# Relative attention: one written order for TensorE, one accumulator for a head, four fold buffers

## What is computed

```python
idx = clip(k - q, -64, 64) + 64                      # 129 relative positions
rk, rv = embK[idx], embV[idx]
logits = einsum('bhqd,bhkd->bhqk', q, k) + einsum('bhqd,qkd->bhqk', q, rk)
w = softmax(logits)
out = einsum('bhqk,bhkd->bhqd', w, v) + einsum('bhqk,qkd->bhqd', w, rv)
x = x + out @ Wo.T + bo
```

## Time and profile before

| | |
|---|---|
| median of 3 runs | 4228.33 us (4212.84 to 4229.1) |
| profiled execution, its own time | 4235.89 us |
| its span | 4234.1 us |
| mean granted TensorE clock | 0.953 |
| PE busy, DVE, ACT, POOL | 92%, 81%, 69%, 35% of the span |

### The profile page before, as it was taken

The page is one execution under the profiler, slowest core; times in us unless marked ns, Lnnn a source line. Parts: engine busy times, 40 slices in busy tenths (PEclk is TensorE's granted clock), DMA queues, the critical chain, the costliest instruction groups (busy, mean ns, idle before and its releaser), DMA issues. The chain is left out here.

```text
span 4234.1 us, 77590 instructions
## 1 busy us (share of the span) xinstructions
PE 3900.7 (92%) x26574; PEld 2061.0 (49%) x26574; DVE 3421.2 (81%) x6363; ACT 2918.5 (69%) x5867; POOL 1485.5 (35%) x1459
## 2 busy tenths in 40 slices
PE   9699999999999999997879999999999999769998
PEld 5255554455544555543533333333333333659998
DVE  7788888888888888880778999999898994557776
ACT  4078777788777887885216777777777777336666
POOL 0356666666666666663100001010000010533233
PEclk9599999999999999998978999999999999779999
DMA  8656666677666666662673334243433331679997
GB/s 309 166 146 171 166 158 160 156 169 171 167 164 164 171 162 165 159 149 86 234 191 53 62 64 72 54 72 61 64 63 63 60 61 41 160 281 325 321 326 223
DMA packets 478603, 635.62 MB, mean 150 GB/s; under 512 B 61320, under 2 KB 404088, under 8 KB 464000
## 3 DMA queue, kind: packets, MB, share of 16 engines
q1 hardware_dynamic: 459680, 607.31, 55.9%
q0 software_dynamic: 18528, 23.34, 2.9%
HBM read 413.23 MB, written 216.19 MB: 149 GB/s over the span
## 5 line engine op out<-in xcount | busy, mean ns | idle before, releaser
L396 DVE TENSOR_REDUCE pa_pm<-pa_psA 128x2 f32<-128x1024 f32 x1024 | 1208.5, 1219 | 136.5 <-PE pa_psA L472 136.3
L1095 ACT ACTIVATE ra_p<-ra_psS 128x512 f32<-128x512 f32 x2048 | 1082.1, 605 | 323.8 <-PE ra_psS L1172 231.6
L444 ACT ACTIVATE pa_p<-pa_psS 128x512 f32<-128x512 f32 x2048 | 1063.8, 603 | 277.4 <-PE pa_psS L490 273.4
L1006 DVE TENSOR_REDUCE ra_pm<-ra_psA 128x1 f32<-128x896 f32 x1024 | 1113.4, 1087 | 162.0 <-PE ra_psA L1130 145.5
L490 PE MATMUL pa_psS<-pa_qs,pa_zs 50*128 50x512 f32 x2048 | 799.4, 467 | 70.9 <-ACT pa_p L444 40.6
L472 PE MATMUL pa_psA<-pa_zs,pa_qs 48*128 48x512 f32 x2048 | 802.8, 475 | 32.8 <-DMA pa_zs<-k_halves 18.2
L1130 PE MATMUL ra_psA<-ra_zs,ra_qs 48*128 48x512 f32 x2048 | 737.0, 454 | 20.6 <-DVE ra_pm L1008 9.9
L1172 PE MATMUL ra_psS<-ra_qs,ra_zs 50*128 50x512 f32 (+3 forms) x2176 | 705.4, 410 | 27.6 <-ACT ra_p L1095 17.9
L490 PEld LDWEIGHTS pa_psS<-pa_qs,pa_zs 50*128 50x128 f32 x2048 | 342.0, 185 | 624.0 <-ACT pa_p L444 611.5
L1203 PE MATMUL ra_psO<-ra_p,ra_vs 128*32 128x512 f32 (+3 forms) x6400 | 557.2, 453 | 0.0
L1172 PEld LDWEIGHTS ra_psS<-ra_qs,ra_zs 50*128 50x128 f32 x2176 | 354.7, 188 | 410.0 <-ACT ra_p L1095 312.7
(11 more groups left out here) (243 smaller groups left out, 4853.6 us busy)
## 6 DMA issues: line engine op xcount, KB each, us to landing
mo_w_parts<-second_weight_parts SPq DMA_DIRECT2D x39, 2048.0 KB, 9.0
relative_rows<-ra_rst SPq DMA_DIRECT2D x128, 512.0 KB, 4.1
ra_blk<-window_rows SPq DMA_DIRECT2D x128, 512.0 KB, 5.0
ra_zs<-k_halves SPq DMA_DIRECT2D x192, 248.0 KB, 7.5
mo_w_raw<-ffn_W SPq DMA_DIRECT2D x39, 1024.0 KB, 11.5
ra_dl<-relative_rows SPq DMA_DIRECT2D x128, 256.0 KB, 5.5
window_rows<-ra_pc SPq DMA_DIRECT2D x128, 256.0 KB, 4.5
pa_qs<-q_halves SPq DMA_DIRECT2D x192, 128.0 KB, 6.5
```

Of the source, the lines that this page charges most:

```text
L396: dve.reduce_max(pm[:, par, 2 * a:2 * a + 2], psA[w][:, :, :], AX.X).then_inc(s_am.h, 1)
L444: act.activation(pr[:, i % NPR, :], psS[:, slot(i), :], ACT.Exp).then_inc(s_ex.h, 1)
L1006: dve.reduce_max(pm[:, q, i, 2 * left:2 * left + 1], psA[w][:, lo:lo + 2 * G - P], AX.X).then_inc(s_far.h, 1)
L1095: act.activation(dst, psS[:, slot(i), :], ACT.Exp if kind == "E" else ACT.Copy).then_inc(s_cp.h, 1)
```

## The change

TensorE's order becomes a written string for each step. `RING` is built from a string of kinds: each step takes four banks of four different chunks, so that column tile c of `psO` belongs to chunk c and adds up over all 16 steps of a head. The last step also multiplies `evc` with `ptr` into the same tiles. `evacuate`, `gather_heads`, `sel`, `ot` and VectorE's `keep_head` go; ScalarE copies `psO` once a head. W and F banks are spread over the head, at 12, 19, 20, 28, 33, 42, 49, 51 and 34, 48, 53, 67. `blk_p` has four buffers, `ob` two; `psS` slots go round by three across heads too. Transfers, joins and folds stand in a new order, those of chunk 0 of head t+1 now in head t.

```diff
-R_STEPS = (1, 2, 3, 5)
-F_STEP = 2
-RTURNS = TURNS + 1 + len(R_STEPS)
-WX_STEPS = (8, 10, 10, 10, 12, 13, 13, 14, 14, 14, 15, 17, 21, 22, 22, 23)
-REL_AHEAD, REL_LEAD = 18, 7
-REL_ORDER = "saasOsaas"
-RC_REL = 30
-SUM_TURNS = (13, 18, 23, 28)
+REL_STEPS = ("sRO", "asasssaaRsssO", "saaassasaasO", "sasasaaO", "saasO", "saasassaO", "assaaasssasaO", "asssaRsO",
+             "saassRO", "asaassasO", "MsssaassaasasaO", "aassaasO", "asassasaO", "aassaasO", "asasssaassasaO",
+             "saasasaOsaas")
+RING_KINDS = "EEEEEEEEEEEEWEEEEEEWWEEEEEEEWEEEEWFEEEEEEEWEEEEEFWEWEFEEEEEEEEEEEEEF"
+WX_AT = (38, 41, 42, 45, 52, 55, 58, 72, 75, 85, 87, 89, 89, 90, 92, 95)
+REL_AHEAD, REL_LEAD = 19, 9
+RC_REL = 7
+SUM_TURNS = ((1, 24), (0, 1), (0, 10), (0, 18))
+RTURNS = TURNS + 4
...
-        blk_p = sb("blk", [P, 2, 4, W])
+        blk_p = sb("blk", [P, 4, 4, W])
-        recb, ob = sb("recb", [P, UN, G]), sb("ob", [P, UN, G])
+        recb, ob = sb("recb", [P, UN, G]), sb("ob", [P, 2, UN, G])
...
@@ SyncE, a head @@
+                    write_p(t, p, 1)
+                    if divide:
+                        store_denominators(t, n)
+                    if third:
+                        write_r(t + 2, p, 0)
+                    read_p(t, p, 1)
+                    if divide:
+                        read_denominators(n)
+                    if third:
+                        write_r(t + 2, p, 1)
+                    if more:
+                        load_stack(t + 1, p + 1, 64, s_qe, STEPS * t)
+                    if p == 2 and third:
                         load_v(t + 2, 4 * (t + 2))
+                    if third:
                         read_r(t + 2, p, 0)
+                    write_p(t, p, 2)
+                    if divide:
+                        store_reciprocals(n)
+                    if third:
                         read_r(t + 2, p, 1)
                     read_p(t, p, 2)
+                    if divide:
                         spread_reciprocals(n)
                     if t + 3 < HEADS:
                         s_am.wait(sp, 32 * (t + 2))
                         load_stack(t + 3, p + 1, 0, s_qa)
+                    write_p(t, p, 3)
+                    if third:
+                        write_r(t + 2, p, 2)
+                        write_r(t + 2, p, 3)
+                    read_p(t, p, 3)
+                    if more:
+                        send_m(t + 1, p + 1)
+                    if third:
+                        read_r(t + 2, p, 2)
+                    if more:
+                        write_p(t + 1, p + 1, 0)
+                    if third:
+                        read_r(t + 2, p, 3)
+                    if more:
+                        read_p(t + 1, p + 1, 0)
+                    if divide:
                         store_o(t, n)
...
@@ GpSimd, a head @@
+                    if more:
                         lay_v(t + 1, p + 1, it + 1 + (p + 1) // U)
+                    join_p(t, p, 2)
+                    fold_p(t, 1)
+                    if third:
                         part_r(t + 2, 0)
                     join_p(t, p, 3)
+                    if third:
                         part_r(t + 2, 1)
+                    fold_p(t, 2)
+                    if more:
+                        join_p(t + 1, p + 1, 0)
+                    fold_p(t, 3)
+                    if p % 2 == 0 and n >= 0:
+                        divide(n)
+                    if third:
                         part_r(t + 2, 2)
                         part_r(t + 2, 3)
+                    if more:
+                        fold_p(t + 1, 0)
+                        join_p(t + 1, p + 1, 1)
...
@@ ScalarE @@
-            def evacuate(t, c):
-                s_us.wait(act, STEPS * t + 4 * c + 4)
-                s_fm.wait(act, t + 1)
-                act.activation(ot[:, c * G:(c + 1) * G], psO[:, :], ACT.Copy).then_inc(s_oev.h, 1)
+            def keep_head(t):
+                s_us.wait(act, STEPS * (t + 1))
+                s_ob.wait(act, 64 * (t // UN - 1))
+                act.activation(ob[:, t // UN % 2, t % UN, :], psO[:, :], ACT.Copy).then_inc(s_nf.h, 1)
...
@@ TensorE @@
-                s_cp.wait(pe, NR * t + before(i) + 1)
+                s_cp.wait(pe, NR * t + i - 2)
...
-                if n == 0:
-                    s_oev.wait(pe, 4 * t + c)
...
                 if k == 0:
                     s_v.wait(pe, 4 * (t + 1))
+                    s_nf.wait(pe, t)
...
+                if k == STEPS - 1:
+                    s_cp.wait(pe, NR * (t + 1))
+                    for c in range(4):
+                        last = pe.matmul(psO[32 * c:32 * c + 32, :], evc[:, :], ptr[:, c * G:(c + 1) * G],
+                                         start=False, stop=True, tile_position=(0, 32 * c), skip_group_check=True)
```

More of the change, by code:

```diff
@@ new lines, with ring_steps @@
+WX_AT = (38, 41, 42, 45, 52, 55, 58, 72, 75, 85, 87, 89, 89, 90, 92, 95)
+REL_AHEAD, REL_LEAD = 19, 9
+RC_REL = 7
+SUM_TURNS = ((1, 24), (0, 1), (0, 10), (0, 18))
+def ring_steps():
+    far, chunk, steps = [0] * 4, 0, []
+    kinds = RING_KINDS.replace("F", "")
+    for k in range(STEPS):
+        now, step = kinds[4 * k:4 * k + 4], []
+        near = [c // 2 for c in range(chunk, chunk + now.count("W"))]
+        others = iter(c for c in range(4) if c not in near)
+        for kind in now:
+            if kind == "W":
+                step.append(("W", chunk // 2, chunk % 2))
+                chunk += 1
+            else:
+                c = next(others)
+                step.append(("E", c, far[c]))
+                far[c] += 1
+        steps.append(step)
+    assert far == [14] * 4 and chunk == 8
+    return steps
@@ L551, with ring @@
+def ring():
+    items = iter(x for step in RING_STEPS for x in step)
+    folded = iter(range(4))
+    return [("F", next(folded), 0) if kind == "F" else next(items) for kind in RING_KINDS]
+RING_STEPS = ring_steps()
+RING = ring()
 NR = len(RING)
-R_STEPS = (1, 2, 3, 5)
-F_STEP = 2
-RTURNS = TURNS + 1 + len(R_STEPS)
-WX_STEPS = (8, 10, 10, 10, 12, 13, 13, 14, 14, 14, 15, 17, 21, 22, 22, 23)
+RTURNS = TURNS + 4
 UN = 2
 LEFT, RIGHT, LEFT_FIRST, RIGHT_LAST = range(4)
-REL_AHEAD, REL_LEAD = 18, 7
@@ L559 @@
-REL_ORDER = "saasOsaas"
-RC_REL = 30
-SUM_TURNS = (13, 18, 23, 28)
 def rel_turns():
[L572 to L583, removed]
+    out, halves, chunk = [], 0, 0
@@ L584, in rel_turns, with rel_attention @@
+    for item in "".join(REL_STEPS):
+        if item == "R":
+            out.append(("R", chunk))
+            chunk += 1
+        elif item == "M":
+            out.append(("M", None))
+        elif item == "a":
+            if halves % 2 == 0:
+                out.append(("A", REL_AHEAD + halves // 2))
+            halves += 1
+    assert len(out) == RTURNS and halves == 64 and chunk == 4
     return out
-def rel_attention(nc, ident, sel, masks, qd, kd, vd, e_stack, evc, ev_side, dr_r, dr_p, den_d, rec_d, ot_rows):
+def rel_attention(nc, ident, masks, qd, kd, vd, e_stack, evc, ev_side, dr_r, dr_p, den_d, rec_d, ot_rows):
@@ L613, in rel_attention @@
     bank_no = {n: k for k, n in enumerate(bank_at)}
[L614 to L617, removed]
+    C0 = REL_LEAD + "".join(REL_STEPS).rpartition("O")[0].count("s") - NR
     wexp_before = {}
[L619 to L624, removed]
+    for j, at in enumerate(WX_AT):
+        wexp_before.setdefault(at % NR, []).append((1 - at // NR, j))
+    early = [j for j, at in enumerate(WX_AT) if at < NR]
     with ExitStack() as ctx:
@@ L707, in released @@
                 s_rc.wait(engine, 4 * (t + 2) + a + 1)
-            elif kind == "F":
-                s_nf.wait(engine, t + 1)
             else:
@@ L828, in _ @@
             send_m(0, 0)
+            s_zd.wait(sp, 16 * NG)
+            write_p(0, 0, 0)
             for c in range(4):
@@ L1053, in _ @@
             s_init.wait(dve, NINIT)
+            for c, (ahead, _) in enumerate(SUM_TURNS):
+                if ahead:
+                    sum_right(0, c)
             for it in range(HEADS // U):
@@ L1277, in rel_projection @@
+def rel_projection(nc, A, ident, masks, e_stack, evc, ev_side, q2, kl2, kr2, v_rows):
     NX = 3
@@ L2526, in program @@
         ident = sb(top, "ident", [P, P])
-        sel = sb(top, "sel", [P, 32])
         with ExitStack() as one:
```

259 lines of the change are left out of this document (100 added, 159 removed).

## The result

The changed kernel takes 4195.09 us (median of 5 runs, 4183.84 to 4198.53), the kernel before in the same comparison 4228.17. The medians are 33 us apart (0.992); the ratio on record is 0.9901, 95% interval 0.9876 to 0.9926, which would be 42 us. So it is faster by about 1%, 33 to 42 us for the 127 forecast, and 0.1 us past the upper end of the forecast's range of 4195. The profiled execution took 4198.53 us (span 4196.8, mean granted clock 0.933 for 0.953).

A forecast was written before the change was run, and what follows sets the result against it. VectorE was taken as the nearest bound, idle 5.64 us a head. 105 us from shorter heads, 20 from late folds and 2 at the stage's end made 127: 4228 to 4101 us, range 4035 to 4195.

The forecast's parts named there:

- the 127 forecast: Whole kernel: 105 us from 30 head intervals, 20 for late folds, 2 at the stage's end.
- What bounds, and the undisturbed head: Relative attention: VectorE is the nearest bound; an undisturbed head falls from 54.3 to 50.8 us, VectorE's work to 47.97.
- the 105 forecast: Relative attention: 30 intervals, each 3.5 us shorter, from 54.3 to 50.8 us.
- two named gaps: VectorE's idle time per head: 0.7 us before keep_head and 2.14 us behind late transposes go; 2.8 stay.
- Late folds: TensorE's 14.4 us of waits in 12 heads for folds on GpSimd before F transposes should go.
- the margins forecast for the folds' transfers: Last window exponential to F: 32 to 57 banks, 25 us for chunk 2, against a fold chain of about 15.
- 20 us for late folds and one clock drop: Disturbed heads: 14.4 us of fold waits and one 5.2 us clock drop go; between 0 and 40.
- the rival that was named: VectorE waits for part_r 0 at head t+2's first turn; one more DMA round trip gives 4369 us; chance 0.05.
- The margin: Relative terms: masks ready at 18 us into a head, VectorE there at 19.3; lateness beyond 1.3 costs VectorE time.
- a rival of its own: Clock: runs without O bring one drop in every head, 5.2 us each, giving 4279 us; chance 0.04.
- The condition that was to show it wrong: Stage: heads above 53 us, VectorE waiting for ra_dl in most heads, or clock below 0.98.
- the 2 us forecast for the last chain: Stage's end: gathering and keep_head, 0.89 + 0.69 us and a wait, fall out of the last chain.

The follow-up runs named there:

- e6: Changed kernel with read_r 0 and chunk 3's fold transfers ahead of SyncE's loads, plus turns and fills spread evenly over the steps: 4323.04 us, ratio 1.0188.
- e1: Changed kernel with read_r 0 issued ahead of the next head's loads and the loads of V: 4185.44 us, ratio 0.9865.
- e9: e5 with VectorE's sum of chunk 1 one turn and an R copy earlier: 4278.13 us, ratio 1.0072.
- e8: e5 with VectorE's sum of chunk 1 four turns later: 4130.30 us, ratio 0.9757.
- e3: e1 with load_stack(t + 1) and load_v moved on behind write_p 2 and read_r 1: 4204.14 us, ratio 0.9918.
- e10: e8 with send_m ahead of load_stack(t + 3) in SyncE's queue and the reciprocals three turns later: 4201.84 us, ratio 0.9876.
- e5: e1 with chunk 3's write_p and read_p ahead of load_stack(t + 3), and load_v at the end of a head's list: 4167.31 us, ratio 0.9827.

## Why the prediction was wrong

**What bounds, and the undisturbed head: right in size.** Forecast 50.8 us with VectorE busy for 47.97; measured 50.35 and 47.3 to 47.7, at 94% (forecast: over 93%). ScalarE's work went from 43.82 to 42.09, three copies of 0.6 less. VectorE's idle time is 3.06 us a head, as forecast (2.8). The late turns' waits of 0.81, 0.38 and 0.95 are gone, the longest is 0.6. (Two slips change nothing: idle times of 1.3 and 4.5 us with the other bounds give 4035 to 4171, not 4040 to 4175; and it is the neighbouring pairs of an E fill and a half turn that rise from 52 to some 61, while the fills in such pairs go from 52 to 49.) Thirty such heads would have given 30 x (54.32 - 50.35) = 119 us for the 105 forecast.

**The cause of it: right only in part.** The prediction took two named gaps off an order that is otherwise the same. e6 has no gathering and no `keep_head` either, and its VectorE stands still for 7.68 us a head, more than the 5.64 of before: with that list, whose neighbours were not fitted to it, the accumulator brought nothing by itself, and the uneven steps all of it. A gap "that goes" was credited without asking whether the new list of steps, evenly spread, would keep the rest.

**Late folds: right.** TensorE's wait for `ra_blk` (14.4 us in 12 heads) is not in the profile after. It came back as soon as e1 moved one transfer and VectorE no longer stood for `ra_dl`, so the margins forecast for the folds' transfers (25 us and more) are not as wide as they were counted: they, too, took a landing for 4.5 to 5 us wherever it stood in SyncE's queue.

**"20 us for late folds and one clock drop": the step that failed, and the rival it belonged to.** The prediction let the disturbed heads lose less than before. They lose more: before (55.23 - 54.32) x 30 = 27 us, after (53.23 - 50.35) x 30 = 86. So 59 us went back, and 119 - 59 is the 60 of the sum above. They went for the most part to the rival that was named, VectorE waiting for the relative terms, with the place right and its price wrong, and with a chance of 0.05. Two terms of its sum were mis-sized:

- *The transfer.* `read_r` 0 was taken at 5.5 us from issue to landing, the median of the earlier trace rows. In the head shown it took 10.2, behind five loads that were issued right before it. The margin was 1.3 us, so the 4.7 more make 3.4 us of wait; 3.68 was measured. And in the heads with V the loads were not five issues of 0.6, but one of 6.01 us besides. A median over all transfers of a name is no price for one that stands behind others. The trace of the kernel before had the right price: there `read_r` 1 stood behind the same five loads and took 8.2 to 11.1 us, 9.1 in the median of 29 heads, while `read_r` 2 took 4.0. With 9.1 for 5.5 the rival's own sum gives, as an estimate, 9.1 - 5.5 - 1.3 = 2.3 us of wait in each head. The Trainium skill (DMA: Bandwidth & Descriptors, Queues, rings and completion order) says that each DMA engine takes descriptors in the order of its ring; the 10.2 us behind the loads agree with it.
- *The clock.* The rival's price counted the wait alone. Of the 86 us, the waits for `ra_dl` are 45.6 at the most (heads that kept their clock lost some 0.5 us less than they waited: 50.89 for a wait of 1.01); most of the other 40 come from the 116 us of half clock, of which 96 stand in heads with such a wait. In the head of 1259.1, 57.18 - 50.36 = 6.8 us are 3.68 of wait and 3.1 for 10.2 us at half clock. Each of the 14 longest of these waits (1.76 to 3.68 us) had a drop within 4 us of its end; the seven others (0.45 to 1.56) had none behind them, and the other two drops stand behind waits of 1.0 and 2.6 us for a join and for TensorE. The prediction had the clock as a rival of its own, set off by runs without O. Beside it it put the rule of the Trainium skill (TensorE: Matmul & The Clock Gate, The HAM clock gate) that activity releases the clock, and took from it that a stage with less standing still has fewer drops. The trace of the changed kernel agrees with the rule, and not with the use made of it: this stage stands still in more heads (21 waits for `ra_dl`, 2 before). The seven heads of e9 show a drop that the waits don't explain.

**The condition that was to show it wrong held:** heads above 53 us in the mean, a wait for `ra_dl` in most heads (21 of 30), a clock of 0.96 in the stage against 0.98.

**The end of the stage and the rest.** Between the last reduction of the stage and the first of the plain attention 5.5 us went (317.8 to 312.4); the 2 us forecast for the last chain may be in them, but some 105 us at half clock lie there too, and the two aren't told apart. The 23.6 us in untouched code, which takes one of two times, were not in the prediction, nor could they be. Without them the span would have fallen by 61 us and not by 37, about half of the 127.

The forecast's 4101 us is near what this order would give undisturbed: e8, from whose profile (span 4150.1) the 30 x 1.4 us above 50.3 a head are taken off, comes to 4108, as an estimate, with the longer of those two times in it. It took three more moves in SyncE's list and one in VectorE's to come to 4130.

## What to carry to other kernels

When a reorder shortens the loop, list for every queue what has to be ready sooner, and price each transfer by its place: what was issued in front of it and for how long the issuing engine stands, not by the median of its name; here the trace before had a transfer at such a place. In a loop that keeps TensorE near full, a stop of one to five microseconds can cost two to three times its length, since half clock can follow it (here 86 us for 45.6, and 134 for 38.7). And change a queue's list one move at a time: here the moves of e1, e3 and e10 each made another transfer late, and the last lost most of what the ones before it had won.

## What the runs showed of the hardware that was not expected

- Stops of about 1 to 5.6 us were followed by 3.4 to 20.5 us at the lower clock: in e9, 13 heads with 38.7 us of waits lost 134. Seven other heads of e9 lost 35 us at the lower clock with no such stop, which is open.
- One load of V held SyncE itself for 4.9 to 6.2 us behind five other loads; the same load took 0.8 to 1.2 ahead of them, in the kernel before, and 1.1 to 1.9 at the end of the list, in e5.
- A transfer of 256 KB, 4.6 us from issue to landing in the median of the profile after, took 10.2 behind five loads of the same queue; in the kernel before another took 8.2 to 11.1 at such a place.
- The untouched part from the plain attention's last row maximum on took 683 to 684 us or 706 to 709; in the longer case the plain attention's last head ran at a granted clock of 0.50 for most of its time.
